# dt stage of a window-attention + selective-scan kernel: GpSimd turns the column-order input once per pair, VectorE's (e-2)e goes first

## What is computed

```python
xs = _cross_scan(xc)                      # x in row order and in column order (and both flipped)
x_dbl = jnp.einsum('bkdl,kcd->bkcl', xs, x_proj_weight)
dts, Bs, Cs = jnp.split(x_dbl, [R_RANK, R_RANK + N_STATE], axis=2)
dts = jnp.einsum('bkrl,kdr->bkdl', dts, dt_projs_weight)
dts = jax.nn.softplus(dts + dt_projs_bias[None, :, :, None])
```

## Time and profile before

| | |
|---|---|
| median of the runs | 21461.23 us |
| profiled execution, its own time | 21461.03 us |
| its span, first to last instruction | 21459.2 us |
| granted TensorE clock, mean over the span | 0.785 |
| busy over the whole span | VectorE 89%, TensorE 76%, GpSimd 71%, ScalarE 47% |
| layer 0 | 0 to about 4390 us |
| dt stage | about 4390 to 6293 us |
| scan and output | the rest |

### The profile page before, as it was taken

How to read it: one execution, slowest core, us unless ns; L and a number is a source line. 1 busy time by engine, 2 the same in 40 slices (tenths; PEclk the granted TensorE clock), 3 DMA queues, 4 the chain that set the end, 5 groups by cost and what they waited for, 6 DMA issues and landing times. The chain is left out here.

```text
span 21459.2 us, 289980 instructions
## 1 busy us (share of the span) xinstructions
PE 16247.2 (76%) x83096; PEld 5502.1 (26%) x83096; DVE 19058.9 (89%) x21113; ACT 10090.7 (47%) x19239; POOL 15280.9 (71%) x5892
## 2 busy tenths in 40 slices
PE   8999999999977777777777777777777777777731
PEld 5555555522211111111111111111111111111111
DVE  5555555589989999999999999999999999999966
ACT  4444444467754444444444444444444444444410
POOL 0000000056669999999999999999999999999977
PEclk9999999989987777777777777777777777777755
DMA  1000000056666666666666666666666666666666
GB/s 22 18 18 18 18 18 18 18 195 226 229 196 129 127 134 131 128 132 130 129 134 131 127 132 132 129 131 131 128 133 133 127 130 133 130 131 133 127 147 166
DMA packets 1129481, 2520.46 MB, mean 117 GB/s; under 512 B 247606, under 2 KB 448824, under 8 KB 1112960
## 3 DMA queue, kind: packets, MB, share of 16 engines
q1 hardware_dynamic: 1128320, 2508.11, 52.3%
HBM read 2000.43 MB, written 507.38 MB: 117 GB/s over the span
## 5 line engine op out<-in xcount | busy, mean ns | idle before, releaser
L1235 POOL TENSOR_TENSOR c_pr<-c_hs,c_c_u 128x1568 f32<-128x1568 f32 x3072 | 9934.9, 3238 | 1037.5 <-DVE c_hs L1199 762.2
L1133 ACT ACTIVATE c_psum<-c_dt_u,c_a_neg 128x784 f32<-128x784 f32 x6144 | 5641.7, 918 | 7475.1 <-DVE c_hs L1199 7422.3
L1199 DVE TENSOR_TENSOR_SCAN c_hs<-c_psum,c_dbx 128x785 f32<-128x785 f32 (+1 forms) x4352 | 7616.3, 1773 | 20.2 <-issue 20.2
L1065 PE MATMUL c_psum<-c_pr,c_red 128*64 128x392 f32 x24576 | 7211.0, 705 | 1.0 <-POOL c_pr L1235 1.0
L1054 PE MATMUL c_psum<-c_br_u,c_sel 48*128 48x512 bf16 (+1 forms) x8704 | 2965.6, 433 | 4029.9 <-DVE c_dbx L1176 3927.8
L1176 DVE TENSOR_TENSOR c_dbx<-c_u_u,c_psum 128x784 f32<-128x784 f32 x4352 | 4103.1, 943 | 40.0 <-PE c_psum L1054 40.0
L1224 POOL TENSOR_TENSOR c_dbp<-c_u_u,c_bp_u 128x784 f32<-128x784 f32 x1792 | 3316.1, 1850 | 105.2 <-DVE c_hs L1199 62.6
L1199 DVE TENSOR_TENSOR_SCAN c_hs<-c_psum,c_dbp 128x785 f32<-128x785 f32 (+1 forms) x1792 | 3191.5, 1781 | 0.0
L196 POOL TENSOR_TENSOR a_xpb<-a_x_sb,a_pb_sb 98x768 f32<-98x768 f32 x128 | 231.2, 1807 | 4063.4 <-DVE a_x L285 4049.3
L1065 PEld LDWEIGHTS c_psum<-c_pr,c_red 128*64 128x64 f32 x24576 | 1789.8, 177 | 3404.6 <-issue 3132.1
L1054 PEld LDWEIGHTS c_psum<-c_br_u,c_sel 48*128 48x128 bf16 x8704 | 522.0, 101 | 8204.3 <-DVE c_dbx L1176 7011.4
(11 more groups left out here) (119 smaller groups left out, 17351.5 us busy)
## 6 DMA issues: line engine op xcount, KB each, us to landing
c_c_u<-scr_bc SPq DMA_DIRECT2D x512, 1568.0 KB, 28.9
c_dt_u<-scr_dt SPq DMA_DIRECT2D x512, 588.0 KB, 7.4
c_u_u<-scr_u SPq DMA_DIRECT2D x512, 588.0 KB, 11.2
c_bp_u<-scr_bc SPq DMA_DIRECT2D x512, 588.0 KB, 22.0
scr_dt<-p_dt_o SPq DMA_DIRECT2D x384, 392.0 KB, 3.0
scr_u<-p_u_o SPq DMA_DIRECT2D x384, 392.0 KB, 2.4
scr_y<-c_y_sb SPq DMA_DIRECT2D x256, 294.0 KB, 17.8
d_yin<-scr_y SPq DMA_DIRECT2D x32, 2352.0 KB, 15.5
```

Of the source, the lines that this page charges most:

```text
L1065: mm = pe.matmul(Y(3 * w + q)[64 * h:64 * h + 64, :], red[:], pr[:, s % RP, HT * h:HT * h + HT], start=(p == 0 and opens(w)), stop=(p == N ...
L1133: nc.scalar.activation(dA(s)[:, data], dt_u[:, d, s // NPR, :], ACT.Exp, scale=a_neg[:, k, s:s + 1]).then_inc(exp_done, 1)
L1199: nc.vector.tensor_tensor_scan(hs[:, s % RH, way], dA(s)[:, way], added, 0.0, ALU.mult, ALU.add).then_inc(scan_done, 1)
L1235: nc.gpsimd.tensor_tensor(pr[:, s % RP:s % RP + 2, :], hs[:, s % RH:s % RH + 2, data], c_u[:, d, s % NPR:s % NPR + 2, :], ALU.mult).then_i ...
```

## The change

On GpSimd a new step `turn` copies, for each pair, the three row blocks of the column-order input out of `xm` into a new tile `xt` (two buffers by turns), where the tokens of column order are consecutive. It runs a pair ahead: three copies of 128 x 784 f32 ahead of the first pair, then one each in the places j = 0, 1 and 3 of every pair for the next. TensorE's products of tiles 3 to 5, the column-order part of the B and C product, and GpSimd's own `times_x` of tiles 3 to 5 read `xt`. TensorE waits ahead of tile 3 for the three copies (`turned`). In `times_x` dt and u are now read and written in their own order. On VectorE `quad` of tile n+1 is put ahead of the first operation of tile n.

```diff
+        xt = sb("xt", [128, 2, 3, CT])
...
-        def order(tile, o, c, h, n):
+        def order(rows, par, k, o, c, h, n):
-            t0 = CT * c + HT * h
             if o == 0:
-                return tile[:, t0:t0 + n]
-            return tile.rearrange("p (r w) -> p w r", r=IMG)[:, t0 // IMG:(t0 + n) // IMG, :]
+                return xm[rows, par, k, CT * c + HT * h:CT * c + HT * h + n]
+            return xt[rows, c % 2, k, HT * h:HT * h + n]
...
+                    if j == TILES // 2:
+                        pe.wait_ge(turned, 3 * (PAIRS * b + c) + 3)
...
+                        at = step(b, n_of(c, j) + 1, last)
+                        if at:
+                            quad(*at)
                         dve.wait_ge(l_done, n + 1)
                         dve.wait_ge(m_done, n + 1)
                         nc.vector.scalar_tensor_tensor(l, m_t[:, j % 2], -0.5, l, ALU.mult, ALU.max).then_inc(p_done, 1)
-                        at = step(b, n_of(c, j) + 1, last)
-                        if at:
-                            quad(*at)
...
-                u = u_o[:, o, k, :]
-                if o:
-                    dt, u = (a.rearrange("p (w r) -> p w r", r=IMG) for a in (dt, u))
-                nc.gpsimd.tensor_tensor(u, dt, order(xm[:, par, k, :], o, c, 0, CT), ALU.mult).then_inc(u_done, 1)
+                nc.gpsimd.tensor_tensor(u_o[:, o, k, :], dt, order(slice(0, 128), par, k, o, c, 0, CT),
+                                        ALU.mult).then_inc(u_done, 1)
+
+            def turn(b, par, c, k):
+
+                g = PAIRS * b + c
+                if k == 0:
+                    if c == 0:
+                        hold(pool, x_in[par], images_in(b, par), fence)
+                    if not (isinstance(g, int) and g < 2):
+                        hold(pool, u_done, TILES * (g - 1), fence)
+                        hold(pool, raw_full, PER * (g - 1), fence)
+                cols = xm[:, par, k, :].rearrange("p (r w) -> p w r", r=IMG)[:, CT * c // IMG:CT * (c + 1) // IMG, :]
+                nc.gpsimd.tensor_copy(xt[:, c % 2, k, :].rearrange("p (w r) -> p w r", r=IMG), cols).then_inc(turned, 1)
...
+                        if j in (0, 1, 3):
+                            if c + 1 < PAIRS:
+                                turn(b, par, c + 1, (0, 1, 3).index(j))
+                            elif not last:
+                                turn(b + 1, 1 - par, 0, (0, 1, 3).index(j))
```

More of the change, by code:

```diff
@@ L614, in build_prep @@
         m_done, p_done, q_done, dt_done = sem("m_done"), sem("p_done"), sem("q_done"), sem("dt_done")
-        u_done = sem("u_done")
+        u_done, turned = sem("u_done"), sem("turned")
         hi_done, rem_done, mid_done, low_done = sem("hi_done"), sem("rem_done"), sem("mid_done"), sem("low_done")
@@ L749, in body @@
                         for h in range(2):
-                            pe.matmul(bank(k, h), wk[:, o, 0, m0:m0 + 128], order(xm[:, par, 0, :], o, c, h, HT),
+                            pe.matmul(bank(k, h), wk[:, o, 0, m0:m0 + 128], order(slice(0, 128), par, 0, o, c, h, HT),
                                       start=True, stop=False)
-                        pe.matmul(bank(k, 0), wk[0:64, o, 1, m0:m0 + 128], order(xm[0:64, par, 1, :], o, c, 0, HT),
+                        pe.matmul(bank(k, 0), wk[0:64, o, 1, m0:m0 + 128], order(slice(0, 64), par, 1, o, c, 0, HT),
                                   start=False, stop=True)
-                        pe.matmul(bank(k, 1), wk[64:128, o, 2, m0:m0 + 128], order(xm[64:128, par, 2, :], o, c, 1, HT),
+                        pe.matmul(bank(k, 1), wk[64:128, o, 2, m0:m0 + 128], order(slice(64, 128), par, 2, o, c, 1, HT),
                                   start=False, stop=True).then_inc(raw_full, 1)
@@ L759, in body @@
                                 pe.matmul(bank(k, h)[64 * o:64 * o + 64, :], wk[:, o, 0, 2 * C:KC],
-                                          order(xm[:, par, 0, :], o, c, h, HT), start=True, stop=False)
+                                          order(slice(0, 128), par, 0, o, c, h, HT), start=True, stop=False)
                             for o in range(2):
                                 mm = pe.matmul(bank(k, h)[64 * o:64 * o + 64, :], wk[0:64, o, 1, 2 * C:KC],
-                                               order(xm[0:64, par, 1, :], o, c, h, HT), start=False, stop=True)
+                                               order(slice(0, 64), par, 1, o, c, h, HT), start=False, stop=True)
                         mm.then_inc(raw_full, 1)
@@ L924, in body @@
                         split(b, PAIRS - 1, part)
+            for k in range(3):
+                turn(0, 0, 0, k)
             halves(pool, body)
```

## The result

| | before | after |
|---|---|---|
| median of 4 runs each | 21461.42 us | 21280.94 us |
| profiled execution, its own time (its span) | 21461.03 (21459.2) | 21279.02 (21277.2) |
| granted TensorE clock, mean over the span | 0.785 | 0.78 |

The ratio is 0.9916, with a 95% interval from 0.9898 to 0.9933: faster by 0.84%, or 182.0 us in the profiled executions. Forecast were 21256 us and a range from 21190 to 21405. The time lies in the range, 25 us above the forecast.

A forecast was written before the change was run, and what follows sets the result against it. VectorE was taken as the bound in the dt stage, with `quad` held up by GpSimd. A pair falling from 29.09 to 25.87 us, times 64, gives 206 us: 21461 - 206 = about 21256 us, range 21190 to 21405.

The forecast's parts named there:

- The bound and the mutual exclusion: dt stage: VectorE bounds; `quad` and any GpSimd operation exclude each other, first to ask goes first; `quad` 2036 ns against 974.
- `quad` first, 3.78 us in a free slot: VectorE: `quad` asks 0.17 us ahead of GpSimd's product, takes 0.84; a dt-to-dt slot with nothing behind the product takes 3.78.
- Dense products and TensorE at 0: Column-order `times_x` falls from 2.24 to 1.85 us; TensorE from 27 to 17.4 us per pair, bounds nothing, booked as 0.
- The copy, c = 1.35: GpSimd's strided copy: dense cast 0.84 us plus a stride surcharge of 0.39 to 0.58, so 1.23 to 1.42, taken as 1.35.
- 21.8 + 3c: Length of a pair in the dt stage, c being one copy's time: three copy slots, two subtraction slots, one free; 25.87 us.
- the slot of a subtraction: Slots behind the products of tiles 1 and 3: the held-up cast goes ahead of the product, 5.06 us each.
- The pace before: dt stage of the kernel before: (6214.87 - 4469.40) / 60 = 29.09 us per pair, 64 pairs.
- A: Rival: the copy on GpSimd is dear, c of 1.6 and over; at 2.1 the total is 21398 us; chance 0.17.
- B: Rival: GpSimd's product goes ahead of `quad` in every slot, 5.70 us from dt to dt, +327 us, 21788; chance 0.09.
- C: Rival: TensorE becomes the bound through its clock, 26.8 us a pair, total 21314 us; chance 0.04.
- D: Rival: casts and subtractions slip into GpSimd's waits for dt, VectorE's own 22.7 us a pair bounds, total 21052; chance 0.04.
- E: Rival: no gain, eaten by something unseen such as a late `turned` wait; within 43 us of 21461; chance 0.04.

The follow-up runs named there:

- e1: Kernel before with only `quad` moved ahead of the tile's first operation, no copies, column-order input still read with a step: 21363.25 us, ratio 0.9954.
- e6: Changed kernel with all four pieces of the bf16 split together at tile 0 of each pair: 21227.06 us, ratio 0.9891.
- e3: Changed kernel with the three copies of a pair reading consecutive numbers, so without the reordering: 21148.45 us, ratio 0.9854 to the kernel before.
- e4: Changed kernel with the three copies of a pair made by ScalarE, behind its clamp of tiles 1, 3 and 5, none by GpSimd: 21297.21 us, ratio 0.9923.
- e11: As e6, but copies read runs of 14 and write with a step, and one of three runs on ScalarE behind tile 3's clamp: 21194.66 us.
- e7: Changed kernel without copies and their wait, column-order products reading consecutive numbers of the input, so without the reordering: 21117.38 us, ratio 0.984.

## Why the prediction was right, and what was off

**The bound and the mutual exclusion: right.** e1 shows `quad` at 1103 ns when no copy stands in its way, and the slots follow the rule that the one that asked first goes first, as at 5009.28, where `quad` ends 0.84 after the copy. Without a memset ahead of `quad` the timelines have no exception to it.

**`quad` first, 3.78 us in a free slot:** right but for 0.18. The one slot with nothing behind the product takes 3.96, with a wait of 0.20 at its dt that the forecast did not have; no run shows where it comes from. The lengths of `quad` came nearly as told: mean 1522 ns (about 1.5), 0.97 in one slot of six, 1.3 to 1.5 behind copies (about 1.2), 2.1 behind subtractions (2.3).

**Dense products and TensorE at 0: right, and needed.** TensorE's four first products of a column-order tile, on its timeline in the changed kernel, and its weight loads of that kind, with what they waited for:

```profile
5001.49 1.58 PE L752 MATMUL p_psum<-p_xt,p_wk 128*128 128x392 f32 x4
```

```profile
L752 PEld LDWEIGHTS p_psum<-p_xt,p_wk 128*128 128x128 f32 x693 | 132.2, 211 | 421.5 <-ACT p_xb L782 265.9 <-POOL p_xt L896 83.8 <-issue 33.1
```

3.13 us became 1.58, as booked, where the granted clock is 1.00. But from 5014.80 to 5017.60 it was 0.52, near the lower of its two levels (1.2 GHz), and four such products with dense reads took 2.90; over the stage TensorE was busy 20.8 us a pair (1210.52 of 1561), not 17.4. That still does not bound the pair, since `quad` waited only 10.4 us in all for ScalarE, and 83.8 us of waits for the copies cost nothing that the runs show: e6 had 226 us of them and was faster. The forecast did not say that without the copies TensorE would be the bound at 28.0 us (e1). It had the row for it, TensorE at 94%: the 0 holds for the whole change, and by it the first part alone would have been priced too well.

**The copy, c = 1.35: the term that was mis-sized.** It takes 1.645 us, 1.60 from start to start, so 3 x 0.25 x 64 = 48 us of gain were missing. With 1.60 the forecast's own 21.8 + 3c gives 26.6 us; 26.56 were measured. What failed was the step from the product: striding its one input added 0.39, and that surcharge was laid on the cast. In a copy the step costs 0.79 (e3), twice as much; that a second input hides part of it in the product fits, but was not tested. The Trainium skill, GPSIMD Engine Reference, section Performance pitfalls for Q7 kernels, spoke for a dear copy. By it a read with a step beyond 8 bytes costs half as much again; by e3 it is 1.9 times, and both durations, 1645 and 859 ns, are below what the page's figures give.

At the cheap end the formula was too dear: for c = 0.84 it had 25.24 us, e3 took 24.32. The timelines of e3 show where: its slots last 3.96, 3.80, 4.10, 4.19, 4.11 and 4.18. The short copy has ended before `quad` asks, and the cast behind it has begun (5016.37, `quad` 5016.74), so that the cast is not held up, and the slot of a subtraction is 4.18, not 5.06.

**The pace before: miscounted.** Between the two rows lie 59 pairs, not 60, so the pace was 29.58 by them and 29.52 over the stage, not 29.09. This hid (29.52 - 29.09) x 64 = 27 us of gain. Counting the instructions in between, 354 of six per pair, would have shown it.

**The loop's turn: not thought of.** The mean pair is 26.83 where an ordinary one is 26.56: 17 us over 64 pairs. A stall that was partly hidden under a slow pace comes out as the pace falls.

**The sum.** 206, + 27 for the miscount, - 44 for the ordinary pair (26.56 in place of 25.87, in the net the three slots of the copies), - 17 for the loop: 172, which is 2.69 x 64. With the first pair, 11.3 earlier and not 2.7, it is 181, of 182 measured. That the forecast came within 25 us is partly luck, two errors of opposite sign: with the pace counted right it would have been 21461 - 233 = 21228, 53 us below the measured time.

**The rivals.** A was the nearest: the copy stands at its border of 1.6, for which the forecast's formula has 21302. B fell: in the ordinary free slot `quad` is 0.16 us ahead and runs first. Its condition was not met, but its mechanism is real: e4 has slots in which `quad` comes too late by hundredths of a microsecond, and they last the 5.7 us that B foretold. C fell: the clock went from 0.91 to 0.87, TensorE is busy 78%, and ScalarE waits for it some 80 us in all (50 ahead of L782, 31 at the B and C output). D fell: a pair of 22.7 was not reached by any order tried, e11 has 24.98, and e7, without copies, 23.71. E fell.

## What to carry to other kernels

When two engines exclude each other, put the shared operation of the faster one right behind the release of the other's, beside work that needs no shared port; then look which third engine was hidden by the loss, since it may cap the gain until it is relieved too. Price a strided one-input copy from a strided one-input row, not from a two-input operation, in which it showed only half of its price; and where no row has it, let the dear bound count for more. Count the instructions between two marks before dividing by a number of periods. An instruction put in as a delay changes what stands ahead of the next one as well as its time: look in the other traces for the same timing without it before drawing a rule.

## What the runs showed of the hardware

- A step of 56 numbers (224 bytes) in a float32 operand costs about a factor of two on three engines: GpSimd's copy of 128x784 took 1645 ns against 859 dense, ScalarE's 1671 against 941 for its dense clamp, TensorE's four 128x392 products 3.13 us against 1.58. On GpSimd a step on the writing side costs nearly the same (1.48 us from start to start against 1.59), though a held `quad` ends 0.20 us earlier.
- Between a VectorE operation with two SBUF inputs and a GpSimd operation, the record that starts first goes first, down to a lead of 0.01 us and a lag of 0.00 (2548 cases in eleven profiles, no exception). Behind a short memset on VectorE the operation still ran first when it started 0.56 us later, at 0.91 us, and was held from 0.68 us on. The Trainium skill, SBUF — State Buffer, section Who interferes with whom, says that the issue order decides who blocks; the trace agrees with it if the beginning of a record is taken for its issue, except behind a memset.
- GpSimd's cast and copy, with one input each, exclude `quad` as its two-input products do (a cast of 0.84 took 1.59, a copy of 1.64 took 2.39 with a held `quad` ahead of it); a VectorE memset was never held, 0.625 us in all 384 records.
